# Matmuls of no use in the idle stretches of TensorE: ahead of the first weights and among the first three batches

## The reference

```python
q = x @ Wq + bq;  k = ctx @ Wk + bk;  v = ctx @ Wv + bv        # layer 0, 32 / 8 / 8 heads of 16
attn = softmax(q k^T / 4 + mask);  out = (attn v) @ Wo + bo
x1 = layernorm(out + x) * gamma + beta
q = x1 @ w_q^T;  k = ctx @ w_k^T;  v = ctx @ w_v^T             # layer 1, one head of 512
result = x1 + alpha * ((softmax(q k^T / sqrt(512)) v) @ w_o^T)
```

## Time and profile before

| | |
|---|---|
| median of three runs | 697.78 us (697.35 to 701.57) |
| the profiled execution | 702.21 us |
| its span | 700.4 us |
| mean granted clock of PE | 0.987 of full speed |
| busy, share of the span | PE 96%, DVE 69%, POOL 58%, ACT 56% |

### The profile page before, as it was taken

How to read it: one execution, slowest core, us unless ns; L and a number is a source line. 1 busy time by engine, 2 the same in 40 slices (tenths; PEclk the granted TensorE clock), 3 DMA queues, 4 the chain that set the end, 5 groups by cost and what they waited for, 6 DMA issues and landing times.

```text
span 700.4 us, 11814 instructions
## 1 busy us (share of the span) xinstructions
PE 670.8 (96%) x3714; PEld 467.6 (67%) x3714; DVE 480.4 (69%) x1419; ACT 390.5 (56%) x589; POOL 405.2 (58%) x257
## 2 busy tenths in 40 slices
PE   7998999999989999999999999999999999999997
PEld 3456756677767777776777777767877767665554
DVE  1539778778676877868686878787786868783220
ACT  2333676656555565766565665666666756576201
POOL 1845766575665656576667556565667565575110
PEclk9999889999999999999999999999999999999999
DMA  8698874666783856767575848586676666623130
GB/s 265 264 175 200 198 126 149 108 186 133 214 169 84 230 126 211 127 196 160 176 173 150 193 131 204 124 223 123 217 129 158 144 175 146 139 92 121 52 112 12
DMA packets 61719, 110.50 MB, mean 158 GB/s; under 512 B 11757, under 2 KB 50221, under 8 KB 61146
## 3 DMA queue, kind: packets, MB, share of 16 engines
q1 hardware_dynamic: 61658, 109.76, 63.8%
HBM read 86.79 MB, written 22.52 MB: 156 GB/s over the span
## 4 chain that ended last, share of the span: by engine, by line
PE 53%; POOL 13%; issue 11%; DMA 11%; DVE 5%; SPq 3%; ACT 2%; POOLq 0%; ACTq 0%; DVEq 0%
POOL pr L2310 8%; PE mx_ps L549 8%; PE work L511 6%; PE work L512 5%; PE work L513 5%; PE o_ps L565 5%; PE work L665 4%; PE work L622 4%; DMA late<-r_dr 4%; DMA qs<-q_dr 3%; PE work L632 2%; PE work L578 2%; PE sc_ps L532 2%; PE sc_ps L536 2%; DVE x L1538 2%
## 5 line engine op out<-in xcount | busy, mean ns | idle before, releaser
L1451 DVE CUSTOM_DVE_ANT_0 mx_ps<-mx_ps,mask_n 100x361 f32<-100x361 f32 x512 | 270.1, 544 | 106.2 <-PE mx_ps L549 102.8
L2310 POOL TENSOR_TENSOR pr<-pr,mask_t 128x800 f32<-128x800 f32 x128 | 243.5, 1908 | 106.7 <-ACT pr L1893 105.4
L549 PE MATMUL mx_ps<-ks,qs 96*100 96x362 f32 x512 | 180.5, 377 | 6.8 <-DMA qs<-q_dr 4.4
L1899 ACT ACTIVATE pr<-pr 128x1200 f32<-128x1200 f32 x128 | 150.0, 1208 | 10.4 <-POOL pr L2310 5.5
L1893 ACT ACTIVATE pr<-sc_ps 128x800 f32<-128x800 f32 x128 | 107.2, 838 | 85.6 <-PE o_ps L565 53.2
L549 PEld LDWEIGHTS mx_ps<-ks,qs 96*100 96x100 f32 x512 | 84.8, 168 | 49.3 <-DVE mx L1451 18.0
L2322 POOL TENSOR_TENSOR c_l<-cT,c_h 128x1448 fp32r<-128x1448 f32 x16 | 53.4, 3340 | 66.4 <-ACT c_h L1920 66.4
L1437 DVE TENSOR_TENSOR pr<-sc_ps,mask_t 128x400 f32<-128x400 f32 x128 | 73.1, 571 | 21.1 <-PE sc_ps L532 17.6
L565 PE MATMUL o_ps<-pr,va 128*32 128x400 f32 (+1 forms) x768 | 71.2, 503 | 1.8 <-ACT pr L1899 1.8
L1451 DVE DVE_READ_ACCUMULATOR2_ANT mx<- 100x1 f32 x512 | 71.7, 140 | 0.0
L632 PE MATMUL work<-n_w,late 128*100 128x512 f32 x128 | 64.5, 593 | 1.0 <-ACT late L1965 0.9
(11 more groups left out here) (122 smaller groups left out, 1155.2 us busy)
## 6 DMA issues: line engine op xcount, KB each, us to landing
qs<-q_dr SPq DMA_DIRECT2D x128, 100.0 KB, 4.1
late<-in_ctx SPq DMA_DIRECT2D x16, 768.0 KB, 4.5
cT<-in_ctxT SPq DMA_DIRECT2D x16, 724.0 KB, 6.3
ks<-k_dr SPq DMA_DIRECT2D x128, 90.5 KB, 3.8
late<-in_ctxT SPq DMA_DIRECT2D x16, 724.0 KB, 6.7
o_dr<-o_s SPq DMA_DIRECT2D x32, 200.0 KB, 4.2
xT<-in_xT SPq DMA_DIRECT2D x16, 200.0 KB, 6.6
q_dr<-q_h SPq DMA_DIRECT2D x16, 200.0 KB, 2.8
```

What stands on the lines that cost most here:

```text
L549: nc.tensor.matmul(mx_ps[0:L, n % 2, 0:SP2], qs[p][0:TERMS, g, L * j:L * (j + 1)], ks[p][0:TERMS, g, 0:SP2], start=True, stop=True).then_i ...
L1451: V.tensor_tensor_reduce(out=src, in0=src, in1=mask_n[p][:, :], scale=1.0, scalar=-3.0e38, op0=ALU.add, op1=ALU.max, accum_out=mx[p][:, n: ...
L1899: A.activation(t, t, ACT.Exp).then_inc(ex_ok, 1)
L2310: G.tensor_tensor(t, t, mask_t[p][:, 1:3, :].unsqueeze(2).to_broadcast([P, 2, J, L]), ALU.add).then_inc(sc_pool, 1)
```

## The change

- `keep_busy` gets two more arguments, a semaphore and a value, waits for these instead of for all maxima, and writes to o_ps, or to bank 1 of sc_ps (where the semaphore is `sc_add`), or to bank 2 (for `fl_ok` at 3). Its weights are from wk_h instead of wq_h, of the same shape.
- New calls in PE's program: 3 + 1 in batch 0's heads, 2 + 1 + 1 + 1 + 4 in batch 1's, 1 + 1 + 2 in batch 2's, 17 matmuls in all.
- A new function `warm_up`, called with 10 ahead of all else on PE: it waits for `zero_ok` at 1 and makes ten fp32 matmuls of `ones` by `ones` (100 by 100) into mx_ps.
- The calls in the tail keep their counts (3, 5, 2, 1, 6, 2, 1, 3, 16, 5, 2, 1, 6, 2, 1) and get new semaphores: os_ok[0] at 16 for the first, sc_add at 128 for the second, os_ok[1] at 16 for the others.

The programs of the other engines and SP's queue are the same as before.

```diff
--- before.py
+++ after.py
@@ -737,11 +737,21 @@
                 turn4(bank(0, xmt_ok, b + 1), lambda j: xm_n[:, P * j:P * (j + 1)], xm_tr)
 
 
-            def keep_busy(count):
-                pe.wait_ge(a_mx, NH * B)
+            def keep_busy(count, free, value):
+                pe.wait_ge(free, value)
+                if free is sc_add:
+                    dst = sc_ps[0:L, 1, :]
+                else:
+                    dst = sc_ps[0:L, 2, :] if free is fl_ok and value == 3 else o_ps[0:L, :]
                 for _ in range(count):
-                    nc.tensor.matmul(mx_ps[0:L, 0, :], wq_h[:, 0, 0:L], wq_h[:, 0, :], start=True, stop=True)
-
+                    nc.tensor.matmul(dst, wk_h[:, 0, 0:L], wq_h[:, 0, :], start=True, stop=True)
+
+            def warm_up(count):
+                pe.wait_ge(zero_ok, 1)
+                for _ in range(count):
+                    nc.tensor.matmul(mx_ps[0:L, 0, 0:L], ones[:, :], ones[:, :], start=True, stop=True)
+
+            warm_up(10)
             fold_m(0, 0, 1)
             fold_m(2, 0, 1)
             fold_m(3, 0, 1)
@@ -800,13 +810,17 @@
             k_part(1, 3, 4)
             heads(0, 14, 15)
             fold_n(3, 3, 4)
-            heads(0, 15, 18)
+            heads(0, 15, 17)
+            keep_busy(3, fl_ok, 3)
+            heads(0, 17, 18)
             turn_maxima(0, 0)
             heads(0, 18, 19)
             v_part(1, 0, 1)
             heads(0, 19, 20)
             v_part(1, 1, 2)
-            heads(0, 20, 22)
+            heads(0, 20, 21)
+            keep_busy(1, fl_ok, 3)
+            heads(0, 21, 22)
             v_part(1, 2, 3)
             heads(0, 22, 24)
             v_part(1, 3, 4)
@@ -850,16 +864,22 @@
             k_part(2, 3, 4)
             heads(1, 15, 17)
             scores(0, 7, 1, 3)
+            keep_busy(2, os_ok[0], 1)
             turn_maxima(1, 0)
             heads(1, 17, 18)
             scores(0, 7, 0, 1)
             v_part(2, 0, 1)
-            heads(1, 18, 20)
+            heads(1, 18, 19)
+            keep_busy(1, os_ok[0], 1)
+            heads(1, 19, 20)
             v_part(2, 1, 2)
-            heads(1, 20, 22)
+            heads(1, 20, 21)
+            keep_busy(1, os_ok[0], 1)
+            heads(1, 21, 22)
             v_part(2, 2, 3)
             heads(1, 22, 24)
             v_part(2, 3, 4)
+            keep_busy(1, os_ok[0], 1)
             scores(1, 0, 1, 3)
             heads(1, 24, 26)
             values(0, 1)
@@ -872,10 +892,12 @@
             heads(1, 30, 31)
             scores(1, 2, 1, 3)
             heads(1, 31, 32)
+            keep_busy(4, os_ok[1], 1)
             turn_maxima(1, 1)
             scores(1, 3, 1, 3)
             heads(2, 0, 2)
             turn_v(2)
+            keep_busy(1, os_ok[1], 1)
             heads(2, 2, 3)
             scores(1, 2, 0, 1)
             heads(2, 3, 4)
@@ -897,6 +919,7 @@
             scores(1, 4, 0, 1)
             scores(1, 5, 1, 3)
             heads(2, 13, 15)
+            keep_busy(1, os_ok[0], 2)
             k_part(3, 0, 1)
             scores(1, 6, 1, 3)
             heads(2, 15, 17)
@@ -907,7 +930,9 @@
             heads(2, 17, 19)
             scores(1, 7, 1, 3)
             k_part(3, 3, 4)
-            heads(2, 19, 22)
+            heads(2, 19, 21)
+            keep_busy(2, os_ok[0], 2)
+            heads(2, 21, 22)
             scores(1, 6, 0, 1)
             y_part(0, 0, 1)
             heads(2, 22, 23)
@@ -1353,36 +1378,36 @@
             d_part(13, 2, 4)
             scores(15, 7, 0, 3)
             y_part(14, 0, 4)
-            keep_busy(3)
+            keep_busy(3, os_ok[0], 16)
             values(15, 1)
             turn_x1(14)
-            keep_busy(5)
+            keep_busy(5, sc_add, 128)
             xm_part(14, 0, 4)
-            keep_busy(2)
...
```

More of the change, by code:

```diff
@@ L1355, in _ @@
             y_part(14, 0, 4)
-            keep_busy(3)
+            keep_busy(3, os_ok[0], 16)
             values(15, 1)
             turn_x1(14)
-            keep_busy(5)
+            keep_busy(5, sc_add, 128)
             xm_part(14, 0, 4)
-            keep_busy(2)
+            keep_busy(2, os_ok[1], 16)
             turn_xm(14)
-            keep_busy(1)
+            keep_busy(1, os_ok[1], 16)
             s1_part(14, 0, 4)
-            keep_busy(6)
+            keep_busy(6, os_ok[1], 16)
             turn_p1(14)
-            keep_busy(2)
+            keep_busy(2, os_ok[1], 16)
             cx_part(14, 0, 4)
-            keep_busy(1)
+            keep_busy(1, os_ok[1], 16)
             d_part(14, 0, 4)
-            keep_busy(3)
+            keep_busy(3, os_ok[1], 16)
             y_part(15, 0, 4)
-            keep_busy(16)
+            keep_busy(16, os_ok[1], 16)
             turn_x1(15)
-            keep_busy(5)
+            keep_busy(5, os_ok[1], 16)
             xm_part(15, 0, 4)
-            keep_busy(2)
+            keep_busy(2, os_ok[1], 16)
             turn_xm(15)
-            keep_busy(1)
+            keep_busy(1, os_ok[1], 16)
             s1_part(15, 0, 4)
-            keep_busy(6)
+            keep_busy(6, os_ok[1], 16)
             turn_p1(15)
-            keep_busy(2)
+            keep_busy(2, os_ok[1], 16)
             cx_part(15, 0, 4)
-            keep_busy(1)
+            keep_busy(1, os_ok[1], 16)
             d_part(15, 0, 4)
```

## The result

The changed kernel takes **707.91 us** (median of 20 runs, 704.87 to 711.51) against 697.78 us (median of 20 runs, 696.46 to 705.38): 10.1 us more, ratio 1.0131 with a 95% interval of 1.0110 to 1.0153 (the ratios here are taken over the single runs and are not the quotients of the medians). That is slower by over 1%, as forecast, and 2.1 us under the 710.0 of the prediction. The profiled execution took 705.75 us, its span 704.0.

The account below looks back on a forecast made before the run. PE, busy 96% of the span, was taken as the bound. 697.78 + 13.0 (start) + 0.9 (dummies) gives 711.7, or 708.3 with 3.4 won back; the middle, 710.0 us, was forecast, range 706.5 to 713.7.

Parts of the forecast that it names:

- The wait, its place and its releaser: PE's head: warm_up waits for POOL's memset of ones behind x_l, so PE starts no earlier than 16.00 instead of 5.08.
- The start term: From PE's start to the heads: the delayed start costs +13.0 us, between +11.2 and +14.4.
- the fold term: Ahead of q_part(0): 22 fold records take 9.46 us, plus 0.3 lost to the low clock level.
- This sub-step: Behind q_part(0), up to 54.00: PE's shrinking waits take in 0.2 us of the delay, at most 1.2.
- The 17 dummies: First batches: 3.9 us of dummies, some 3.0 covered by PE's idle time, so +0.9 stays open.
- The win of 3.4 us: At 98.20: dummies right before the clock fall keep the high level, giving back 3.4 us in the profiled execution.
- the two forms of the sum: Whole kernel: 711.7 if the median run lacks the fall at 98, 708.3 if it has it.
- Its own sign of being wrong: Whole kernel: wrong if, among other signs, the shift at 44.89 shrinks towards 200 us.
- The fall at 67.46 and the tail: No win counted at 67.46, as no dummy stands in its gap; the tail's edits cost nothing, some tenths if uncovered.
- (a): PE's head: the wait is met early and the change works, 694.7 us, at most 690 without falls; 3%.
- (b): Behind the start: later PE idle that does not hang on PE takes the delay in, 702 us; 6%.
- (c): Batches: the dummies' cover is gone and PE falls to the low level once more, 716.1 us; 8%.

Follow-up runs that it names:

- warm-up-only kernel: The kernel before plus warm_up(10) and nothing else of the change: 709.00 us, ratio 1.0154.
- wait-only: The kernel before plus one PE wait for zero_ok at 1 ahead of the first fold_m, no matmul added: 707.56 us, ratio 1.0130.
- doubled kernel: The changed kernel without warm_up, each group of the 17 dummies doubled to make 34: 697.63 us, ratio 0.9969.
- the kernels that have only the one or only the other: Changed kernel with constants() ahead of x_low(0) but without the 17 dummies: 0.9988; changed kernel without warm_up: 0.9964 and 0.9997.
- the five kernels without the four: Before, wait-only, warm-up-only, the tail's edits alone (0.9993), and ones written first without the 17 dummies (0.9988); the four are dummies ahead of turn_maxima(1, 1).
- four only: The changed kernel without warm_up and the 17 dummies, but with the four ahead of turn_maxima(1, 1) put back: 698.52 us, ratio 0.9997.
- 5 more: The changed kernel with constants() ahead of x_low(0), the last m_l made earlier on DVE, and five more dummies in batch 0's heads: 696.10 us, ratio 0.9940.
- ones first: The changed kernel with constants() ahead of x_low(0) in POOL's program: 693.99 us, ratio 0.9931.
- no warm-up: The changed kernel without warm_up(10), all else kept: 697.00 us (0.9964), and again on another chip 698.09 us (0.9997).

## Why the prediction came out as it did

**The wait, its place and its releaser: right.** PE starts on the warm-up's line, released by POOL's `ones`, and neither x_l nor anything ahead of it moved with PE. The wait alone costs 9.5 us of the 10.1.

**The start term: +13.0 predicted, +11.4 measured at the heads.** Its parts: PE started at 15.52 and not at 16.05, since x's chain on ACT and POOL ran 0.5 us earlier in this execution (15.85 in the warm-up-only kernel, 15.39 in the wait-only one); the ten matmuls took 3.44 us and not 3.8, next to the lower bound of 3.3 that went by columns; the 22 fold records 9.62 against 9.76. That makes 12.20 at q_part(0) instead of 13.2. That the fold term fits so well is partly luck. The first four fold records take 2.29 us (18.96 to 21.25) where four at full pace take 1.72, so 0.57 is lost to the slow pace and not 0.3, and without that the 22 take 9.05 us and not 9.46, since q_part(0)'s first record starts (28.58) before the last fold records are through (29.14). The same holds before, where the slow start cost 2.3 us and not the 1.84 of the prediction (5.08 to 8.65 for four records, then 1.27 for two):

```profile
8.65 1.43 PE L674 MATMUL o_ps<-pr 128*128 128x512 f32 x2
9.92 1.02 PE L674 MATMUL sc_ps<-pr 128*128 128x512 f32 x2
```

Then 0.84 us came back by the heads, where I had taken 0.2: the wait for the stacks shrank from 0.69 to 0.27 us, and from q_part(0) to the heads PE idles 0.33 of 27.67 us, where it idled 0.92 of 28.51. This sub-step was under-sized, and why is open. The transfers did shift with PE: the first load of the stacks is issued 3.70 us behind the store of k, 3.74 before. The DMA traffic in this stretch is lighter (95 GB/s against 238), but it is as light in the wait-only kernel (86), and there the wait for the stacks is 0.87 us and the heads are later than q_part(0) by another 0.40. In the warm-up-only kernel 1.26 came back. So this term moves by over a microsecond from one execution to the next. The bound of 1.2 held for the changed kernel.

**The 17 dummies: +0.9 predicted, small and covered.** Right in kind; no run shows a cost of the 17. The doubled kernel's median speaks for more cover than I counted, its profile for at most a little more (1.5 to 2.9 of the second 3.9 us are open).

**The win of 3.4 us: right in mechanism, too large for a median.** 2.85 us came back at that place in the profiled pair. But the low stretch comes only in some executions, so against medians it is 1 to 2 us at most, and the two runs without the warm-up measure 1.1 and 0.3 us against before. Between 711.7 and 708.3, the two forms of the sum, the second was nearer; with the measured start term and a win of about 1 the sum comes to the median: 697.78 + 11.4 = 709.2, less about 1. The prediction took it, without a row, that the low stretches are what differs between executions; the recorded clocks bear that out (last section). Its own sign of being wrong, a shift that shrinks towards 200 us, came in form: 11.36 at the heads, 7.85 at 198. Of these 3.5 us 2.85 are the win it forecast, so only some 0.7 were taken in.

**The fall at 67.46 and the tail: right.** The low stretch is there (78.2 to 85.0) as none of the new dummies stands in its gap, and the tail is 52.50 against 52.39 us.

**The rivals.** (a) The other side needed `zero_ok` before about 1.3 us; with POOL's two calls exchanged it came at 0.73 to 0.91, and 694.7 was forecast, 693.99 measured. Its condition is what the change lacks. That the number fits is luck in part: its 0.6 for the start and 2.5 for the dummies should show one by one, and the kernels that have only the one or only the other gain 0.6 us (0.9988) and 0.3 to 1.1. (b) Of the delay at the heads 0.4 us was taken in by values 1, and the wait-only kernel's median, 9.5, lies 1.6 under its 11.1 at q_part(0), 2.0 under the 11.5 at its heads: little, as forecast. (c) did not occur.

The Trainium skill's rule (TensorE: Matmul & The Clock Gate, Part 1) that activity releases the throttle agrees with the starts of all kernels: whatever comes first on PE, fold records or dummies, runs at the slow pace. Activity helped only where something useful did not have to wait for it.

## What to carry to other kernels

Before a filler is put at the head of an engine, ask for the first instruction that raises the semaphore it waits on, and read in the trace of the kernel as it is when that instruction runs: here a 0.18 us memset stood on another engine's queue behind work that waited 13 us for a load, and one wait on it cost 9.5 us. A filler's operand must be ready before the work it is to bridge to, so move its maker to the head of its queue too: the changed kernel with that one exchange is 4 us faster than before instead of 10 slower, though most of the 4 is not the warm-up's. A filler at the head also has to last until the work comes: 1.43 us of idle time behind it, and the work began at the slow pace all the same. Dummies in waits are nearly free as long as the waits last (17 of them here; 34 by the median, 1.5 to 2.9 us of cost by the profiles), and cost their full time beyond that (68).

## What the runs showed of the hardware

- An fp32 matmul of 100 by 100 ones takes two records of 0.172 us at the lower clock level, in step with its columns (a 512-column record takes 0.87, so 100 columns 0.170); the 128 weight columns of the dearer neighbour were not the measure. In this stretch PEld is busy as long as PE (3.44 of 3.44 us).
- The granted clock in the record is 1.00 from the start on, although the first records run at half pace in every kernel; it is to be read only from its first fall on.
- x_l takes 1.87 to 2.25 us at the start, in the kernels whose start is shown here, and 1.03 later. The summary of its line before (shortest, median, longest in ns):

```profile
L2316 POOL TENSOR_TENSOR x_l<-xT,x_h x16: 1030/1035/2092, 13.7 to 551.8; 128x400 fp32r<-128x400 f32 x16
```

  At the start it runs beside DVE's split of wq (2.29 us of DVE); that the two hinder each other is argued, not shown.
- Whether the clock falls at a given sparse place differs from execution to execution: between values 2 and 3 it does in three of the five kernels without the four, and the mean granted clock of before lies anywhere from 0.984 to 0.998. In step with that goes the time: over the 23 runs of before on chip a, which lie 10 us apart, the mean granted clock and the time have a correlation of -0.80, and a thousandth less clock goes with 0.7 us more, which is what PE loses by it. Chip b (30 runs) gives -0.78 and 0.6 us, chip c (27 runs) -0.81 and 0.8; two more runs on c, with clocks of 0.943 and 0.947 at 703.70 and 701.74 us, don't fit and are left out. By the squares of these, some three fifths of the scatter of before go with the clock. Late transfers are a part of that: each of the low stretches that the profiles show behind 200 us (at 211 in before, 438 in "four only", 510 in "5 more", 513 in "ones first", 608 in "no warm-up") begins within 3 us of a wait of PE for a stack transfer, of 0.8 to 3.2 us.
